# Cross attention on one core: the row maximum of a score tile in the first pass, as one VectorE instruction over 128x1024 instead of two over 128x512

## The chip, the cores and the metric

The kernel runs on one core of one Trainium2 chip. The metric is the device time of one execution in microseconds (us), the median of the runs shown. A core has TensorE (PE; its weight loads are shown apart, as PEld), VectorE (DVE), ScalarE (ACT), GpSimd (POOL) and SyncE (SP, which here only issues DMAs), each with an instruction queue of its own that is worked through in order. Waits between engines are semaphore waits.

## The reference, cut to what matters

For 8 batches of 256 rows, 1024 wide, with 32 heads of 32 columns:

```python
mu, var = mean(x), var(x)                       # over the last axis
z = (x - mu) * rsqrt(var + 1e-5) * gamma + beta
Q = split_heads(z @ Wq.T)
K = V = split_heads(ctx)                        # ctx has 256 rows too
scores = einsum('bhsd,bhtd->bhst', Q, K) * 32 ** -0.5    # masked
probs = softmax(scores)
attn = einsum('bhst,bhtd->bhsd', probs, V)
out = x + merge_heads(attn) @ Wout.T
```

## The kernel before, in words

Every matmul input but the probabilities is split into two f16 parts, and products are made from three partial ones (PASSES). The batches b0 to b7 are worked through one after the other. The work of a batch is two passes over the scores.

**The first pass** finds, for every row of scores, the logarithm of its sum of exponentials. It has 16 steps (STEPS). In step n, TensorE makes one score tile of 128 query rows x 4 heads x 256 keys (scores_s, matmuls at L588) in the PSUM tensor score[n % 2], so there are two buffers. VectorE finds the maximum of each row and head (max_step, L912 to L918), negated, into nmax. ScalarE takes the exponential of the tile with nmax as bias and accumulates the sums, one ACTIVATE for each of the 4 heads, each followed by an ACTIVATION_READ_ACCUMULATOR (row_sums, L733 to L741). The last of them releases sum_done, and scores_s of step n+2 waits for it at L582 before it overwrites the buffer.

**What fills TensorE between score tiles** is written out by hand. From b1 on, behind the scores of each step stand 7 matmuls of the output projection of the batch before (o_matmuls, L560, 128x512 each; 6 in b7), and near the end of the pass some of the query projection of the next batch (q_matmuls, L514, 128x256 each): 4 in step 13, 18 in step 14, and 38 behind the scores of step 15. In b0 there are query projections and the transposes of Wout (wo_transposes, L477; ScalarE's part of them is L724, VectorE's L832).

**VectorE's other work in the first pass**: the residual adds of the output (add_residual, L962) behind the maxima of steps 5, 8, 11 and 14; lse_half in step 10; and lse_rows, five dependent small instructions (L943 to L951), behind the maximum of step 12. They turn the sums of the first 8 steps into three rows of l_rows, which SyncE's queue puts into q_stack by DMA (fill_l_rows, L262). In that queue they stand behind loads, stores and the DMA transposes of the next batch (turn_z L230, turn_k L237).

**The second pass** makes the transposed scores with the logarithm already in the matmul (scores_t, L614), so that one ACTIVATE over 128x1024 gives the probabilities (exp_step, L761), then the product with V (probs_times_v, L626) and its split (att_split: L769 on ScalarE, L955 on VectorE). Its first two tiles wait for sum_done of steps 14 and 15 and for the DMAs of l_rows.

max_done counts the maxima: two per step, so row_sums waits for it ahead of head 0 and ahead of head 2 (L737, L738), and lse_half for all of its half (L923).

Of the kernel before, what the change touches and what calls it, by code (L numbers as in the profile page):

```python
# [13 lines left out]
AX = mybir.AxisListType  # L14
# [19 lines left out]
STEPS = G * ST  # L34
# [14 lines left out]
def xattn(nc, x, ctx_in, mask, wq, wout, gamma, beta, out):  # L49
    es = ExitStack()  # L50
    with es:
        def sb(name, shape, dt):
            return es.enter_context(nc.sbuf_tensor(name, shape, dt))

        def sem(name):
            return es.enter_context(nc.semaphore(name))
# [18 lines left out]
        nmax = sb("nmax", [P, ST, 2, J, HALF], F32)  # L75
# [58 lines left out]
        score = [es.enter_context(nc.psum_tensor(f"score{i}", [P, J, S], F32)) for i in range(2)]  # L134
# [26 lines left out]
        s_ready, max_done, sum_done = sem("s_ready"), sem("max_done"), sem("sum_done")  # L161
# [532 lines left out]
        def _(act):  # L694
# [38 lines left out]
            def row_sums(b, n):  # L733
                g, st = n // 2, n % 2
                h, gl = divmod(g, HALF)
                for j in range(J):
                    if j % 2 == 0:  # L737
                        act.wait_ge(max_done, b * 2 * STEPS + 2 * n + j // 2 + 1)  # L738
                    last = act.activation(score[n % 2][:, j, :], score[n % 2][:, j, :], ACT.Exp, bias=nmax[:, st, h, j, gl:gl + 1],  # L739
                                          accum_out=sums[:, st, h, j, gl:gl + 1])  # L740
                last.then_inc(sum_done, 1)  # L741
# [29 lines left out]
            def iteration(b, first, last):  # L771
                for n in range(STEPS):
                    if first and n in Q0_SPLITS:
                        q_split(0, Q0_SPLITS[n])
                    if first and n == Q1_SPLIT:
                        q_split(1, 0)
                    row_sums(b, n)
                    if first:
                        wo_split(n)
                    if n == STEPS // 2:  # L780
                        ln_sums(b, 0)
                    if n == STEPS // 2 + 1:
                        exp_ln(b, 0)
                ln_sums(b, 1)
                exp_ln(b, 1)
                splits = Q_SPLITS_FIRST if first else Q_SPLITS
                for g in range(G):
                    if not last and g in splits:
                        q_split(b + 1, splits[g])
                    exp_step(b, 2 * g, first, last)  # L790
                    exp_step(b, 2 * g + 1, first, last)
                    if g >= 2:
                        att_split(b, g - 2, first)
                att_split(b, G - 2, first)
                if not last:
                    q_split(b + 1, 3)
                att_split(b, G - 1, first)
# [21 lines left out]
        def _(dve):  # L819
# [92 lines left out]
            def max_step(b, n):  # L912
                g, st = n // 2, n % 2
                h, gl = divmod(g, HALF)
                dve.wait_ge(s_ready, b * STEPS + n + 1)
                for j2 in range(2):
                    at = slice(2 * j2, 2 * j2 + 2)
                    dve.tensor_reduce(nmax[:, st, h, at, gl], score[n % 2][:, at, :], AX.X, ALU.max, negate=True).then_inc(max_done, 1)  # L918


            def lse_half(b, h):
                at = b * 6 + 3 * h
                dve.wait_ge(max_done, b * 2 * STEPS + (h + 1) * STEPS)  # L923
                dve.wait_ge(ln_done, b * 2 + h + 1)
                dve.scalar_tensor_tensor(out=lse_t[:, :, h], in0=nmax[:, :, h], scalar=1.0, in1=ln_s[:, :, h], op0=ALU.mult, op1=ALU.subtract).then_inc(lse_step, 1)
                dve.wait_ge(le_done, b * 2 + h + 1)
                dve.scalar_tensor_tensor(out=lse_r[:, :, h], in0=sums[:, :, h], scalar=1.0, in1=ln_e[:, :, h], op0=ALU.mult, op1=ALU.mult).then_inc(lse_step, 1)
                dve.wait_ge(lse_step, at + 2)
                for st in range(ST):
                    last = dve.scalar_tensor_tensor(out=lse[:, st, h], in0=lse_t[:, st, h], scalar=1.0, in1=lse_r[:, st, h], op0=ALU.add, op1=ALU.subtract)  # L930
                last.then_inc(lse_step, 1)
# [33 lines left out]
            def iteration(b, first, last, more):  # L965
                adds = O_ADDS_LAST if last else O_ADDS
                for n in range(STEPS):
                    max_step(b, n)
                    if first and n in Q0_SPLITS:
                        q_split(0, Q0_SPLITS[n])  # L970
                    if first and n == Q1_SPLIT:
                        q_split(1, 0)
                    if first and n == 0:
                        centre(1, 0)
                    if first and n in (1, 2):
                        normalise(1, n - 1)
                    if first and n > 0:
                        wo_split(n - 1)
                    if not first and n in adds:
                        if adds.index(n) == 0:  # L980
                            if known(b, 1):
                                dve.wait_ge(k_in[1], 4 * DMA)
                            else:
                                for i in range(2):
                                    dve.wait_ge(out_done[i], (b - 1) * 2 * DMA)
                        add_residual(b - 1, adds.index(n))
                    if n == STEPS // 2 + 2:
                        lse_half(b, 0)
                    if n == L_STEP + 1:
                        lse_rows(b, 0)  # L990
# [3 lines left out]
                if first:  # L994
                    wo_split(STEPS - 1)
                lse_half(b, 1)
                for g in range(G):
                    if not last and g in splits:
# [83 lines left out]
```

## Time and profile before

| What | Value |
|---|---|
| Median of 3 runs | 584.61 us (583.23, 584.61, 587.07) |
| The profiled execution's own time | 582.48 us |
| Its span, first to last instruction | 580.6 us, so 1.9 us lie around it |
| PE busy (matmul) | 547.9 us, 94% of the span |
| ACT busy | 427.0 us, 74% |
| DVE busy | 370.3 us, 64% |
| POOL busy | 186.7 us, 32% |
| Mean granted TensorE clock | 0.994 of full speed |

The profile is of one execution, with times from the start of its span. A row of the timeline reads: start in us, length in us, engine, line of the kernel, operation, output <- inputs, shapes, how many instructions are merged in the row (x4), and in brackets the idle time of the engine before it with what ended it. Matmuls are pipelined, and the ends of their rows are modelled.

### The profile page before, as it was taken

What the parts mean: (1) busy time and instruction counts of PE and PEld (TensorE: products, weight loads), DVE (VectorE), ACT (ScalarE), POOL (GpSimd) and SP (SyncE); (2) the same over time, 40 slices, a digit from 0 to 9 for tenths busy, and PEclk for the clock granted to TensorE, in tenths of its full rate; (3) what the DMA queues carried; (4) which work ended last, traced back from release to release, by engine and by line L of the source; (5) the groups of instructions that cost most, each with busy time, mean ns of one, the idle gap of its engine ahead of it and who ended that gap; (6) DMA issues with size and microseconds to landing.
All of it is one profiled execution on the core that took longest, in us unless ns stands there. A gap on an engine that the chain in (4) does not pass through costs nothing.

```text
span 580.6 us, 12070 instructions
## 1 busy us (share of the span) xinstructions
PE 547.9 (94%) x4529; PEld 364.7 (63%) x4529; DVE 370.3 (64%) x751; ACT 427.0 (74%) x1322; POOL 186.7 (32%) x239
## 2 busy tenths in 40 slices
PE   1898799999999999999999999999999999999897
PEld 1787676556775577656775577656775577644443
DVE  4979687677647757478565857468565762278311
ACT  1469787698668975698668976598767986599850
POOL 0856530770047400590046400590036500030000
PEclk9999799999999999999999999999999999999999
DMA  8978992399128952299126972299325943031103
GB/s 311 314 190 232 246 197 85 96 218 207 39 73 143 226 144 80 68 233 237 45 73 133 225 153 76 42 200 258 87 73 126 221 93 89 24 91 56 58 2 109
DMA packets 122634, 80.90 MB, mean 139 GB/s; under 512 B 102000, under 2 KB 103568, under 8 KB 122576
## 3 DMA queue, kind: packets, MB, share of 16 engines
q1 hardware_dynamic: 119120, 73.84, 53.5%
q0 software_dynamic: 3456, 6.30, 6.0%
q8 instruction: 36, 0.59, 0.4%
q14 instruction: 22, 0.18, 0.1%
HBM read 34.61 MB, written 8.39 MB: 74 GB/s over the span
## 4 chain that ended last, share of the span: by engine, by line
PE 67%; SPq 8%; DVE 8%; POOL 6%; DMA 5%; ACT 4%; issue 2%; DVEq 0%
PE mm L514 21%; PE mm L560 15%; PE pv L626 11%; PE score L614 10%; PE score L588 6%; SPq L237 6%; ACT score L739 3%; DVE nmax L918 2%; PE mm L539 2%; PE score L539 2%; POOL probs L404 2%; DMA l_rest<-in_mask_BxS_bf 1%; DMA q_stack<-l_rows 1%; DMA ctx_sb<-in_ctx 1%; POOL probs L401 1%
## 5 line engine op out<-in xcount | busy, mean ns | idle before, releaser
L739 ACT ACTIVATE score<-score,nmax 128x256 f32<-128x256 f32 x512 | 230.0, 463 | 26.9 <-DVE nmax L918 26.0
L918 DVE TENSOR_REDUCE nmax<-score 128x2 f32<-128x512 f32 x256 | 164.2, 685 | 46.6 <-PE score L588 45.6
L514 PE MATMUL mm<-zT,wqT 128*128 128x256 f16 x1536 | 184.9, 273 | 1.6 <-DVE l_rows L951 1.1
L761 ACT ACTIVATE probs<-score 128x1024 f32<-128x1024 f32 x128 | 123.9, 1022 | 74.0 <-PE score L614 74.0
L514 PEld LDWEIGHTS mm<-zT,wqT 128*128 128x128 f16 x1536 | 149.8, 98 | 24.3 <-issue 4.2
L560 PE MATMUL mm<-woT,aT 128*128 128x512 f16 x672 | 161.5, 379 | 0.0
L739 ACT ACTIVATION_READ_ACCUMULATOR score<-score,nmax 128x1 f32 x512 | 113.6, 222 | 0.0
L560 PEld LDWEIGHTS mm<-woT,aT 128*128 128x128 f16 x672 | 65.4, 97 | 58.5
L588 PE MATMUL score<-k_stack,q_stack 97*128 97x256 f16 x512 | 78.6, 276 | 7.4 <-DMA q_stack<-qT 4.3
L955 DVE TENSOR_TENSOR aT<-pv,aT 128x256 f16<-128x256 f32 x64 | 26.9, 423 | 91.1 <-ACT aT L769 90.0
L378 POOL CAST z_nat<-x_nat 128x1024 f16<-128x1024 f32 x12 | 12.4, 1036 | 210.7 <-DVE x_nat L909 210.7
L588 PEld LDWEIGHTS score<-k_stack,q_stack 97*128 97x128 f16 x512 | 48.0, 98 | 39.4 <-issue 9.4
L614 PE MATMUL score<-q_stack,k_stack 100*128 100x256 f16 x512 | 67.8, 274 | 4.0 <-DMA q_stack<-l_rows 2.9
L626 PE MATMUL pv<-probs,ctx_sb 128*32 128x256 f32 x1024 | 68.5, 385 | 0.2 <-DVE aT L955 0.2
L411 POOL DMA_DIRECT2D q_stack<-qT x84 | 41.2, 498 | 75.8 <-DVE qT L847 75.6
L614 PEld LDWEIGHTS score<-q_stack,k_stack 100*128 100x128 f16 x512 | 45.4, 98 | 31.2 <-issue 17.7
L626 PEld LDWEIGHTS pv<-probs,ctx_sb 128*32 128x32 f32 x1024 | 26.9, 109 | 24.9 <-ACT probs L761 7.6
L731 ACT ACTIVATE qT<-mm 128x512 f16<-128x512 f32 x32 | 19.4, 608 | 14.2 <-PE mm L514 14.2
L769 ACT ACTIVATE aT<-pv 128x256 f16<-128x256 f32 x64 | 24.8, 390 | 6.6 <-PE pv L626 6.6
L847 DVE SCALAR_TENSOR_TENSOR qT<-mm,qT 128x512 f16<-128x512 f32 x32 | 22.1, 690 | 11.7 <-ACT qT L731 11.0
L404 POOL TENSOR_TENSOR probs<-ctx_sb,probs 128x512 f16<-128x512 f32 x24 | 27.5, 1148 | 0.0
L380 POOL TENSOR_TENSOR z_nat<-x_nat,z_nat 128x1024 f16<-128x1024 f32 x12 | 25.6, 2131 | 1.0
(96 smaller groups left out, 367.3 us busy)
## 6 DMA issues: line engine op xcount, KB each, us to landing
ctx_sb<-in_ctx SPq DMA_DIRECT2D x8, 1024.0 KB, 5.8
res<-in_x SPq DMA_DIRECT2D x32, 256.0 KB, 3.2
out<-o_buf SPq DMA_DIRECT2D x32, 256.0 KB, 2.5
x_nat<-in_x SPq DMA_DIRECT2D x6, 1024.0 KB, 6.0
q_stack<-qT SPq DMA_DIRECT2D x84, 64.0 KB, 2.0
q_stack<-qT POOLq DMA_DIRECT2D x84, 64.0 KB, 7.7
woT<-in_L_xattn_Wq SPq DMA_DIRECT2D x8, 512.0 KB, 12.5
probs<-in_L_xattn_Wout SPq DMA_DIRECT2D x8, 512.0 KB, 4.2
```

What stands on the lines that cost most here:

```text
L237: sp.dma_start_transpose(k_turned(pa, c), k_nat(a, c).rearrange("p n d -> p (n d)")).then_inc(k_in[c // 2], DMA)
L404: pool.tensor_tensor(to[:, :, 2 * DH:3 * DH], of, to[:, :, 0:DH], ALU.subtract).then_inc(k_done, 1)
L411: pool.dma_start(q_stack[DH * r:DH * (r + 1), 1, j], qT[DH * j:DH * (j + 1), part, HALF:G, :]).then_inc(q_in[1], DMA)
L514: last = pe.matmul(mm[i % 2][:, m2 * S:(m2 + 1) * S], wqT[:, wp, k, m * P:(m + 1) * P], zT[:, zp, k, :], start=(v2 == 0), stop=(v2 == KT * ...
L560: last = pe.matmul(mm[i % 2][:], aT[:, ap, k, st * P:(st + 1) * P], woT[:, wp, k, nh * 512:(nh + 1) * 512], start=(v == 0), stop=(v == O_M ...
L588: last = pe.matmul(score[n % 2][:, j, :], q_stack[0:S_ROWS, h, j, gl, st * P:(st + 1) * P], k_stack[0:S_ROWS, pb, h, gl, j, :], start=True ...
L614: last = pe.matmul(score[n % 2][:, j, :], k_stack[0:T_ROWS, pb, h, gl, j, tt * P:(tt + 1) * P], q_stack[0:T_ROWS, h, j, gl, :], start=True ...
L626: last = pe.matmul(pv[g % 2][DH * j:DH * (j + 1), 0, :], ctx_sb[:, pb, tt, g * P + DH * j:g * P + DH * (j + 1)], probs[:, g % 2, tt, j, :] ...
L739: last = act.activation(score[n % 2][:, j, :], score[n % 2][:, j, :], ACT.Exp, bias=nmax[:, st, h, j, gl:gl + 1], accum_out=sums[:, st, h, ...
L761: act.activation(probs[:, g % 2, tt], score[n % 2][:], ACT.Exp).then_inc(exp_done, 1)
L918: dve.tensor_reduce(nmax[:, st, h, at, gl], score[n % 2][:, at, :], AX.X, ALU.max, negate=True).then_inc(max_done, 1)
L955: dve.tensor_tensor(aT[:, 1, g, :], pv[g % 2][:, 0, :], aT[:, 0, g, :], ALU.subtract).then_inc(a_lo, 1)
```

## The change

The two reductions of a step become one over the whole tile. max_done then counts one per step, ScalarE waits once per tile ahead of head 0, and lse_half's count is halved.

```diff
             def row_sums(b, n):
                 g, st = n // 2, n % 2
                 h, gl = divmod(g, HALF)
+                act.wait_ge(max_done, b * STEPS + n + 1)
                 for j in range(J):
-                    if j % 2 == 0:
-                        act.wait_ge(max_done, b * 2 * STEPS + 2 * n + j // 2 + 1)
                     last = act.activation(score[n % 2][:, j, :], score[n % 2][:, j, :], ACT.Exp, bias=nmax[:, st, h, j, gl:gl + 1],
                                           accum_out=sums[:, st, h, j, gl:gl + 1])
                 last.then_inc(sum_done, 1)
...
                 dve.wait_ge(s_ready, b * STEPS + n + 1)
-                for j2 in range(2):
-                    at = slice(2 * j2, 2 * j2 + 2)
-                    dve.tensor_reduce(nmax[:, st, h, at, gl], score[n % 2][:, at, :], AX.X, ALU.max, negate=True).then_inc(max_done, 1)
+                dve.tensor_reduce(nmax[:, st, h, :, gl], score[n % 2][:], AX.X, ALU.max, negate=True).then_inc(max_done, 1)
 
 
             def lse_half(b, h):
                 at = b * 6 + 3 * h
-                dve.wait_ge(max_done, b * 2 * STEPS + (h + 1) * STEPS)
+                dve.wait_ge(max_done, b * STEPS + (h + 1) * STEPS // 2)
```

## Rows read from the trace of the kernel before

**Rows 1.** Busy time by engine, first pass of b3 (243.3 to 278.0 us)

```profile
core 0: us, PE busy (x) PEld busy (x) DVE busy (x) ACT busy (x) POOL busy (x), PEclk, DMA share, GB/s
243.30:278.00 34.70, 34.52 (x225) 21.36 (x222) 26.43 (x50) 31.65 (x134) 16.55 (x24) 1.00 1.01 213
```

**Rows 2.** Timeline, a steady step of b3's first pass and the step after next

```profile
256.98 0.60 PE L588 MATMUL score<-k_stack,q_stack 97*128 97x256 f16 x4
...
257.62 1.29 DVE L918 TENSOR_REDUCE nmax<-score 128x2 f32<-128x512 f32 x2 [0.66 <-PE score L588]
...
258.35 0.45 ACT L739 ACTIVATE score<-score,nmax 128x256 f32<-128x256 f32 x1
...
260.06 0.21 ACT L739 ACTIVATION_READ_ACCUMULATOR score<-score,nmax 128x1 f32 x1
...
260.67 0.53 PEld L588 LDWEIGHTS score<-k_stack,q_stack 97*128 97x128 f16 x4
...
260.88 0.60 PE L588 MATMUL score<-k_stack,q_stack 97*128 97x256 f16 x4
```

**Rows 3.** Groups of instructions by shape, whole kernel (count, busy us, mean ns)

```profile
L739 ACT ACTIVATE score<-score,nmax 128x256 f32<-128x256 f32 x512 | 230.0, 463 | 26.9 <-DVE nmax L918 26.0
L918 DVE TENSOR_REDUCE nmax<-score 128x2 f32<-128x512 f32 x256 | 164.2, 685 | 46.6 <-PE score L588 45.6
...
L761 ACT ACTIVATE probs<-score 128x1024 f32<-128x1024 f32 x128 | 123.9, 1022 | 74.0 <-PE score L614 74.0
...
L955 DVE TENSOR_TENSOR aT<-pv,aT 128x256 f16<-128x256 f32 x64 | 26.9, 423 | 91.1 <-ACT aT L769 90.0
```

**Rows 4.** Timeline, start of b3's first pass: maxima of step 0, scores of step 2

```profile
244.20 1.28 DVE L918 TENSOR_REDUCE nmax<-score 128x2 f32<-128x512 f32 x2
...
247.22 0.60 PE L588 MATMUL score<-k_stack,q_stack 97*128 97x256 f16 x4
```

**Rows 5.** Timeline, steps 13 to 15 of b3's first pass

```profile
270.91 2.47 DVE L918 TENSOR_REDUCE nmax<-score 128x2 f32<-128x512 f32 x4
...
271.62 0.45 ACT L739 ACTIVATE score<-score,nmax 128x256 f32<-128x256 f32 x1 [1.37 <-DVE nmax L918]
...
273.34 0.21 ACT L739 ACTIVATION_READ_ACCUMULATOR score<-score,nmax 128x1 f32 x1
...
273.60 0.33 PEld L588 LDWEIGHTS score<-k_stack,q_stack 97*128 97x128 f16 x4 [0.46 <-ACT score L739]
...
274.05 4.31 PE L514 MATMUL mm<-zT,wqT 128*128 128x256 f16 x38
```

**Rows 6.** Timeline of PE, from the first pass to the second, b1

```profile
141.02 4.31 PE L514 MATMUL mm<-zT,wqT 128*128 128x256 f16 x38
145.44 1.05 PE L614 MATMUL score<-q_stack,k_stack 100*128 100x256 f16 x8
```

**Rows 7.** Timeline of PE, from the first pass to the second, b6

```profile
471.92 4.31 PE L514 MATMUL mm<-zT,wqT 128*128 128x256 f16 x38
476.07 1.04 PE L614 MATMUL score<-q_stack,k_stack 100*128 100x256 f16 x8
```

**Rows 8.** Chain that ended last: start us, us, what; end of b0's and of b7's first pass

```profile
76.12 1.93 ACT score L739 x8
...
83.93 1.93 ACT probs L761 x2
...
533.29 5.58 ACT score L739 x24
```

**Rows 9.** Timeline of b7's first pass: maxima of step 0, scores of steps 2 and 12, logarithm

```profile
507.44 1.28 DVE L918 TENSOR_REDUCE nmax<-score 128x2 f32<-128x512 f32 x2
...
510.14 0.61 PE L588 MATMUL score<-k_stack,q_stack 97*128 97x256 f16 x4
...
528.62 0.60 PE L588 MATMUL score<-k_stack,q_stack 97*128 97x256 f16 x4
...
538.89 0.23 ACT L745 ACTIVATE ln_s<-sums 128x32 f32<-128x32 f32 x1
```

## The prediction, made before the changed kernel was run

> **What bounds the kernel now.** I read the page first (TensorE busy 94% of the span, so the question is where TensorE will wait), then the busy time by stretch, the timeline of one step, and the chain that ended last. In the first pass of b3 TensorE is busy 34.52 of 34.70 us, ScalarE 31.65, VectorE 26.43 [rows 1]: TensorE is the bound, ScalarE is close behind, VectorE has room. The reader is to see in the timeline that the three form a loop. The scores of a step start at 256.98, the maxima 0.64 later at 257.62, ScalarE at 258.35, 0.73 after them and thus as soon as the first of the two is done; the step's last accumulator read ends at 260.27, and the scores two steps on, which need that buffer, start at 260.88 with a weight load at 260.67 [rows 2]. So two steps take 3.90 us on TensorE, and the buffer is free 0.40 us before the weight load. That is the slack of the loop that the change draws on.
>
> **The new instruction.** The trace has no reduction over 1024. The one over 512 takes 685 ns [rows 3]; two back to back end 1.29 us after the first began [rows 2], so the second adds 0.605. From 256 to 512 columns VectorE grows from 423 to 685 ns [rows 3], 262 per 256, so 1024 gives 0.685 + 2 x 0.262 = 1.21 us. That beats the pair (1.29) by 0.08 us: per step VectorE gains that. Bounds: below, ScalarE's instruction over 128x1024 takes 1.02 [rows 3]; above, two full durations, 1.37. I take 1.21, since it extends the same engine's own rows.
>
> **What it adds.** ScalarE now waits for all of the maxima. Its start moves from 0.73 to 1.21 + 0.05 = 1.26 after the maxima begin: 0.53 later (bounds 0.34 and 0.69). Behind that wait stand the four ACTIVATEs of the step, and for the last of them the scores two steps on. The removed second wait gains nothing: it never held ScalarE, whose starts in a tile are 0.45 us apart throughout.
>
> **The loop, anew.** From ScalarE's start to the end of its last read is 260.27 - 258.35 = 1.92 us [rows 2]. Where TensorE had to wait, the weight load followed the last read by 0.05 (273.34 + 0.21 to 273.60 [rows 5]), the scores start with it (0.01 later), and the maxima begin 0.64 after the scores [rows 2], together 0.65. Two steps need 1.26 + 1.92 + 0.05 + 0.65 = 3.88 us. TensorE's own work gives 3.90. The loop is just covered in b1 to b6, and in b7, where a step has 6 filling matmuls and takes 1.82 to 1.84 us because of ScalarE, it is not. The places one by one:
>
> *Start of b1 to b6.* VectorE comes late to step 0, from the end of the batch before. Maxima at 244.20, so the buffer is free at 244.20 + 1.26 + 1.92 + 0.05 = 247.43, against scores that start at 247.22 [rows 4]: +0.2 per batch.
>
> *Steady steps, b1 to b6.* 3.88 against 3.90: nothing by the sum, but a weight load that comes that late is no longer hidden behind the matmul in front. I put 0.1 for a batch.
>
> *Steps 13 to 15, b1 to b6.* Here ScalarE already waits, 1.37 us, because lse_rows holds VectorE; and TensorE waits for ScalarE, 0.46 for the weight load at 273.60 [rows 5]. Nothing covers ScalarE's later start. Less the 0.05 to 0.08 that step 12's cheaper maximum gives back: +0.48. The end of ScalarE's sums also comes later, by 0.3 more, but behind the scores of step 15 TensorE has 38 matmuls (4.15 us), 1.5 us more than ScalarE needs. Hidden.
>
> So each of b1 to b6 loses 0.8 us on TensorE. Part of it was lost anyway: the second pass starts when l_rows is in q_stack, and in b1 TensorE was ready at 141.02 + 4.15 = 145.17 but started at 145.44 [rows 6], while in b6 it started at 471.92 + 4.15 = 476.07 without a wait [rows 7]. The same subtraction for the six batches gives waits of 0.27, 0.99, 0.38, 1.21, 0.14 and 0. SyncE's queue sets these; in the timeline it goes from one transpose to the next since the batch began and waits for none of VectorE's work that moves, so its end stays. Each delay is swallowed up to its wait: left are 0.5, 0, 0.4, 0, 0.7 and 0.8, together 2.4 us of 4.8.
>
> *b0.* VectorE itself sets its first steps; 3 maxima there and 2 later give 0.08 each back, 0.3 or 0.4. From step 13 the chain runs through ScalarE to the first probabilities (76.12 to 83.93) [rows 8], where the later start counts in full, 0.53. Net +0.2.
>
> *b7.* Step 0's maxima begin at 507.44, so the scores of step 2 start at 507.44 + 1.26 + 1.92 + 0.06 = 510.68 and not 510.14: +0.54. From step 2 to step 12 are five pairs: 5 x 3.88 = 19.40 against 528.62 - 510.14 = 18.48 [rows 9]: +0.9. At step 13 the chain goes through VectorE to ScalarE: +0.53, less 0.08. After that ScalarE did three tiles in one run (24 instructions, 5.58 us) [rows 8]; step 15 now needs sums of 13, scores, maxima, so its sums start 3.88 after those of 13, not 3.60: +0.3. Together +2.2, and the logarithm at 538.89 [rows 9] and all behind it move by that; nothing later in b7 absorbs it, as the second pass of b7 hangs on it.
>
> Sum: 0.2 + 2.4 + 2.2 = +4.8 us. The profiled execution's own 582.48 (span 580.6 and 1.9 around it) becomes 587.3. It lies 2.1 under the median of the runs, so the median 584.61 becomes 589.4.
>
> **A rule weighed.** The rows show VectorE not full (26.43 of 34.70) and ScalarE's start hanging on the first half-result [rows 1, 2]. The Trainium skill speaks to both sides in Perfetto Trace Analysis, section Optimizing Scalar/DVE Operations: grouping into larger operations helps where the engine is saturated; where it isn't, but causes bubbles on others, splitting lets work finish sooner. The trace agrees with the second for the steps of this pass; by the first, 128 x 0.08 = 10 us of VectorE's time would be the gain. That is the faster rival below, and its condition doesn't hold by these rows.
>
> **The rivals.**
> (a) *Every pair of steps waits.* If the late weight load costs 0.1 to 0.2 us for each pair, or the reduction takes 1.37, the loop is 4.0 to 4.05. Six pairs in six batches at 0.15 add 5.4; the swallowed part grows only to 3.0 in all. Time: +8 to +11, 593 to 596. For: the margin is 0.02 us, ScalarE gets 0.24 more in steps 8 and 9 and has only 0.14 us of room per step (1.95 less 4 x 0.45). Against: the one place where TensorE waits shows a restart at once.
> (b) *Hidden.* SyncE's chain ends later than in this execution (it moves by a us between batches) or the reduction takes nearer 1.02; then b1 to b6 lose next to nothing and b7 some 1 to 2: +1 to +2.5, 585.6 to 587.
> (c) *Faster.* VectorE is the real bound where it matters: if its end of step, not ScalarE's start, releases what is late, each of 128 steps gains up to 0.08: -10 us at most, and some -6 (578.5) if b1 to b6 alone do so. It decides where VectorE reaches the next maxima after the scores are ready. For: so it is in b0's first steps and behind lse_rows in step 12. Against: VectorE sat 45.6 us waiting for scores before these maxima [rows 3].
>
> **Chances.** Forecast, +3 to +7: 0.53. (a) 0.22, (b) 0.20, (c) 0.05. A measurement of this kernel can tell about 1% from no change, 5.8 us, up to 590.5. The forecast lies under it for some two thirds, (b) wholly, (a) not at all. So faster by over 1% 0.04, within 1% 0.58, slower by over 1% 0.38. The bounds of the reduction carried through the same sum give +1.4 (1.02) and +10.9 (1.37), so 586.0 to 595.5; the range is 585.6 to 595.
>
> **What would show it.** 128 reductions of some 1.21 us in place of 256 of 0.685, and VectorE's busy time for them down from 164 to 155 us. ScalarE's first ACTIVATE 1.26 after the maxima begin; its idle time behind nmax up from 26.9 us [rows 3]. In b1 to b6 the weight load of step 15 about 0.95 late against 0.46, the scores of step 2 0.2 later, the steps between still 1.95 apart; waits for l_rows shorter in b2 and b4. In b7 steps of 1.94. Wrong would be: steps of 1.98 or more in b1 to b6 (a), a first pass of b7 not longer (b), or score tiles that start earlier than before (c).

## The result, and the profile after

The changed kernel takes 588.35 us (median of 20 runs, 586.31 to 592.41) against 583.12 for the kernel before (20 runs); the ratio is 1.0083, 95% interval 1.0064 to 1.0102. So it is slower by 5.2 us, where +4.8 was forecast (588.35 us for 589.4). A ratio, here and below, leaves out single executions more than 1.5% above the fastest of their kernel, and is not the exact quotient of the medians. Its profiled execution took 589.48 us with a span of 587.6, 7.0 more than the span of before.

Groups of instructions of the changed kernel, from its page (count | busy us, mean ns | idle before them); they answer to [rows 3]:

```profile
L738 ACT ACTIVATE score<-score,nmax 128x256 f32<-128x256 f32 x512 | 229.5, 452 | 33.1 <-DVE nmax L915 29.7
L915 DVE TENSOR_REDUCE nmax<-score 128x4 f32<-128x1024 f32 x128 | 156.0, 1222 | 57.0 <-PE score L588 54.9
...
L588 PE MATMUL score<-k_stack,q_stack 97*128 97x256 f16 x512 | 78.6, 276 | 11.5 <-ACT score L738 6.7
...
L588 PEld LDWEIGHTS score<-k_stack,q_stack 97*128 97x128 f16 x512 | 43.3, 98 | 50.8 <-ACT score L738 32.1
```

The reduction over 1024 takes 1.222 us (1.21 was estimated), and VectorE's busy time for the maxima falls from 164.2 us [rows 3] to 156.0. None of it is gained: VectorE's idle time before the maxima rises by more, from 46.6 [rows 3] to 57.0. The weight loads of the score tiles now wait 32.1 us for ScalarE (8.9 in the kernel before), but most of that is hidden, as the weight load runs while TensorE is still busy with the matmuls in front. What costs time shows in the third line: the matmuls themselves stand idle for ScalarE for 6.7 us, where it was 2.2 us in the kernel before.

A steady step of b3's first pass, from the timeline of the changed kernel; it answers to [rows 2]:

```profile
250.28 0.60 PE L588 MATMUL score<-k_stack,q_stack 97*128 97x256 f16 x4
...
250.92 1.23 DVE L915 TENSOR_REDUCE nmax<-score 128x4 f32<-128x1024 f32 x1 [0.72 <-PE score L588]
...
252.18 0.45 ACT L738 ACTIVATE score<-score,nmax 128x256 f32<-128x256 f32 x1
...
254.17 0.34 PEld L588 LDWEIGHTS score<-k_stack,q_stack 97*128 97x128 f16 x4 [0.32 <-ACT score L738]
254.19 0.60 PE L588 MATMUL score<-k_stack,q_stack 97*128 97x256 f16 x4
```

ScalarE starts 252.18 - 250.92 = 1.26 us after the maxima begin (0.73 in [rows 2]). The weight load two steps on has moved from 0.21 ahead of its matmul to 0.02, yet the scores start 3.91 us after those two steps before: the loop just closes.

The two places of b1 to b6 where it doesn't, again in b3, timeline of the changed kernel; they answer to [rows 4] and [rows 5]:

```profile
245.08 1.22 DVE L915 TENSOR_REDUCE nmax<-score 128x4 f32<-128x1024 f32 x1
...
248.32 0.61 PE L588 MATMUL score<-k_stack,q_stack 97*128 97x256 f16 x4
```

```profile
272.04 0.60 PE L588 MATMUL score<-k_stack,q_stack 97*128 97x256 f16 x4
...
273.27 0.45 ACT L738 ACTIVATE score<-score,nmax 128x256 f32<-128x256 f32 x1 [1.30 <-DVE nmax L915]
...
275.25 0.33 PEld L588 LDWEIGHTS score<-k_stack,q_stack 97*128 97x128 f16 x4 [0.93 <-ACT score L738]
275.26 0.61 PE L588 MATMUL score<-k_stack,q_stack 97*128 97x256 f16 x4 [0.65 <-ACT score L738]
```

At the start the scores of step 2 come 248.32 - 245.08 = 3.24 us after the maxima of step 0, against 3.02 in [rows 4]. From step 14 to 15 it takes 3.22 us, and the weight load of step 15 waits 0.93 us against 0.46 [rows 5].

The distances of the score tiles, taken from the same timeline rows for every batch (us):

| | step 1 to 2 | 7 to 8 | 14 to 15 | other steps | step 0 to 15 |
|---|---|---|---|---|---|
| before, b1 to b6 | 1.95 | 1.95 | 2.75 | 1.95 | 30.3 |
| changed, b1 to b6 | 2.17 | 2.03 | 3.22 | 1.95 | 31.07 |
| before, b7 | 1.84 | 1.91 | 3.03 | mostly 1.82 | 28.72 |
| changed, b7 | 2.38 | 2.17 | 3.23 | mostly 1.83, 2.07 by turns | 30.83 |

("Step n to n+1" is from scores to scores; 12 comes 0.2 later in each for the two transposes before it.) Step 7 to 8 of b2 is left out, since there TensorE stood still for another reason, below.

Where the 7.0 us of the two spans come from, by the start of each batch's scores: -1.2 before b0's first scores, +0.5 in b0 (74.12 against 73.57), +3.9 in b1 to b6 (400.15 against 396.27), +2.4 in b7 to the logarithm (34.70 against 32.34), +1.4 behind it (43.12 against 41.68).

The last of these was in no term of the forecast. PE's timeline of the changed kernel, second pass of b7:

```profile
547.52 1.94 PE L626 MATMUL pv<-probs,ctx_sb 128*32 128x256 f32 x16
549.39 1.61 PE L614 MATMUL score<-q_stack,k_stack 100*128 100x256 f16 x8
```

Busy time of the changed kernel in two stretches (columns as in [rows 1]):

```profile
547.40:549.40 2.00, 2.00 (x18) 0.61 (x18) 0.71 (x2) 1.25 (x2) 0.00 (x0) 0.50 0.01 2
540.00:544.00 4.00, 2.52 (x14) 1.20 (x14) 2.21 (x3) 3.86 (x18) 0.00 (x0) 1.00 0.20 72
```

TensorE's granted clock is 0.50, the lower of its two levels (1.2 GHz), from about 547.4 on, and the 16 matmuls of the product with V take 1.94 us there and 1.07 elsewhere. Before that, from 540 to 544, TensorE was busy 2.52 of 4.00 us at full clock. But so it was in the kernel before: there it was busy 2.52 of the 4.00 us up to the logarithm (534.9 to 538.9), and no fall followed.

### The profile page after: what moved, and what is told of

The parts are those of the page before. It is cut to its first block, busy times and chain, and to the rows that moved or that the text cites. A ratio compares the mean times of both kernels' runs of the same rounds, so it can differ in the third digit from the quotient of the medians.

```text
span 587.6 us, 11942 instructions
## 1 busy us (share of the span) xinstructions
PE 551.7 (94%) x4529; PEld 360.5 (61%) x4529; DVE 363.1 (62%) x623; ACT 429.5 (73%) x1322; POOL 186.7 (32%) x239
## 4 chain that ended last, share of the span: by engine, by line
PE 59%; DVE 9%; POOL 9%; SPq 9%; ACT 7%; DMA 5%; issue 2%; DVEq 0%
PE mm L514 21%; PE pv L626 11%; PE score L614 10%; PE mm L560 9%; SPq L237 7%; ACT score L738 5%; PE score L588 4%; DVE nmax L915 4%; POOL probs L404 2%; POOL probs L401 2%; POOL q_stack L411 2%; PE mm L539 2%; PE score L539 2%; DMA ctx_sb<-in_ctx 1%; DMA l_rest<-in_mask_BxS_bf 1%
## 5 line engine op out<-in xcount | busy, mean ns | idle before, releaser
L915 DVE TENSOR_REDUCE nmax<-score 128x4 f32<-128x1024 f32 x128 | 156.0, 1222 | 57.0 <-PE score L588 54.9
L738 ACT ACTIVATION_READ_ACCUMULATOR score<-score,nmax 128x1 f32 x512 | 107.1, 209 | 0.0
L588 PEld LDWEIGHTS score<-k_stack,q_stack 97*128 97x128 f16 x512 | 43.3, 98 | 50.8 <-ACT score L738 32.1
```

The lines of the kernel that those rows point to most:

```text
L588: last = pe.matmul(score[n % 2][:, j, :], q_stack[0:S_ROWS, h, j, gl, st * P:(st + 1) * P], k_stack[0:S_ROWS, pb, h, gl, j, :], start=True ...
L915: dve.tensor_reduce(nmax[:, st, h, :, gl], score[n % 2][:], AX.X, ALU.max, negate=True).then_inc(max_done, 1)
```

## The experiments

All are built from the kernel before or the changed one. They ran on three chips (g4 on a fourth), e1 5 times, e4 6, g3 8 and the others 12 times; each ratio is against the kernel before on the same chip (medians there 582.29, 582.65 and 581.95). "By the medians" below is the plain difference to these.

**e1_pair_one_wait.** Two reductions, one wait of ScalarE for both:

```diff
                 for j in range(J):
-                    if j % 2 == 0:
-                        act.wait_ge(max_done, b * 2 * STEPS + 2 * n + j // 2 + 1)
+                    if j == 0:
+                        act.wait_ge(max_done, b * 2 * STEPS + 2 * n + 2)
```

> Two reductions of 512 as before, but ScalarE waits for both ahead of head 0. My theory (the loss is ScalarE's later start, not the wide instruction): ScalarE starts 1.34 us after the maxima begin, 0.08 later even than with the wide instruction, so two steps need 3.96 us against 3.90 of TensorE's work. Score tiles of b1 to b6 now come 0.06 later per pair of steps, the step after 14 is 3.3 long, b7's first pass is 0.4 longer still than the changed kernel's. Time: 2 us or so over the changed kernel, +6 to +9 over the kernel before. Rival (the instruction over two banks, or its length on VectorE, costs by itself): the kernel before's time, within 1 us.

591.12 us, ratio 1.0161 (1.0128 to 1.0194), +8.8 us by the medians. A step of b3, from its timeline:

```profile
249.32 1.29 DVE L918 TENSOR_REDUCE nmax<-score 128x2 f32<-128x512 f32 x2 [0.66 <-PE score L588]
...
250.65 0.45 ACT L739 ACTIVATE score<-score,nmax 128x256 f32<-128x256 f32 x1
250.67 0.33 PEld L588 LDWEIGHTS score<-k_stack,q_stack 97*128 97x128 f16 x4 [0.38 <-ACT score L739]
```

ScalarE starts 1.33 us after the maxima begin. Every second step is now 2.00 us, the last one 3.30, and a first pass of b1 to b6 takes 31.48. With the very instructions of the kernel before, and only the wait moved, the loss is larger than the change's own. So it comes from when ScalarE starts, not from the wide instruction; and a start 0.07 us later than with the wide one was enough to take the loop over its edge.

**e3_wide_covered, e4_wide_b7, e5_wide_0_13.** Three parts of the change, each alone. Here max_done was raised by the number of heads that a reduction covers:

```diff
+        def max_parts(b, n):
+            return (4,) if 1 <= b < B - 1 and n not in (0, 13) else (2, 2)
...
-                    dve.tensor_reduce(nmax[:, st, h, at, gl], score[n % 2][:, at, :], AX.X, ALU.max, negate=True).then_inc(max_done, 1)
+                    dve.tensor_reduce(nmax[:, st, h, at, gl], score[n % 2][:, at, :], AX.X, ALU.max, negate=True).then_inc(max_done, part)
```

(b == B - 1 in e4, 1 <= b < B - 1 and n in (0, 13) in e5.)

> The wide reduction only in b1 to b6, and there not in steps 0 and 13; pairs elsewhere. Theory: the loop's 3.88 us lies just inside TensorE's 3.90, so only step 8 (where ScalarE's logarithm stands) gives 0.08 per batch: +0 to +0.5 over the kernel before, score tiles 1.95 apart. Rival (each pair of steps pays for the late weight load): +3 or more. Rival (VectorE's saved time pays): -2 or lower.

> The wide reduction only in b7. Theory: b7's first pass up to the logarithm takes 2.4 us longer, as in the changed kernel, and nothing else moves; in addition TensorE's granted clock falls to half for some 3 us behind it, as in the changed kernel's profile, for 1.5 more: +2.4 to +3.9. If the halved clock in that profile was chance and has nothing to do with the longer waits of TensorE there: +2.4. Rival (the loss is in b1 to b6 alone): +0.

> The wide reduction only in steps 0 and 13 of b1 to b6. Theory: 0.2 and 0.47 us on TensorE in each of the six batches, 4.0 in all, of which the wait for the rows of l_rows swallows a part: +1.5 to +3 over the kernel before. Rival (swallowed wholly, as SyncE's queue is the bound there): +0 to +0.5. Together with the other two parts it makes the changed kernel's +5.2 if the parts add.

In this order: 584.35 us, ratio 1.0034 (1.0009 to 1.0059); 588.92, 1.0131 (1.0090 to 1.0172); 584.81, 1.0047 (1.0024 to 1.0071). These don't tell the parts apart, because they brought a change of their own: also where two reductions stood, the maxima began 0.71 us after the scores and not 0.64. From the timeline of e4_wide_b7, b3, where it should be the kernel before:

```profile
248.19 0.60 PE L591 MATMUL score<-k_stack,q_stack 97*128 97x256 f16 x4
...
248.90 1.29 DVE L925 TENSOR_REDUCE nmax<-score 128x2 f32<-128x512 f32 x2 [0.66 <-PE score L591]
```

In e3 this made every second steady step 2.00 us. They are a second sight of the edge that e1 showed: with 0.07 us more in the loop, here ahead of the maxima and there behind them, it is longer than TensorE's work.

e5 lies in its range (+2.5 us by the medians); e3 doesn't (+2.1, for +0.5 at most), by its steps of 2.00 us. e4 was slower than any of its expectations: +6.6 us by the medians, where at most +3.9 was expected. Its profiled execution, at 585.54 us the fastest of the six, has 35.16 us in b7 up to the logarithm and a halved clock behind it, and its span is 3.0 us longer than that of before. Why the other five took 588 to 594 us no trace shows; f1 below, the same part with increments of one, doesn't repeat it.

**g4_pair_inc2.** The kernel before with every increment of max_done and every wait on it doubled, one execution:

```diff
-                    dve.tensor_reduce(nmax[:, st, h, at, gl], score[n % 2][:, at, :], AX.X, ALU.max, negate=True).then_inc(max_done, 1)
+                    dve.tensor_reduce(nmax[:, st, h, at, gl], score[n % 2][:, at, :], AX.X, ALU.max, negate=True).then_inc(max_done, 2)
```

> The kernel before with max_done raised by two per reduction and all waits on it doubled; nothing else. If the 0.07 us more from scores to maxima in the runs with increments above one comes from the increment, it is here too: 0.71 us and not 0.64, and 128 more instructions in the profile (12198). Rival (it came from the mixed widths of those kernels): 0.64 and 12070. In time no difference that one execution can show.

585.25 us beside 578.95, one run each, which settles nothing about time (its b5 held one stall of 3.4 us, below). What the increment does is plain in its timeline:

```profile
251.67 0.60 PE L588 MATMUL score<-k_stack,q_stack 97*128 97x256 f16 x4
252.38 1.29 DVE L918 TENSOR_REDUCE nmax<-score 128x2 f32<-128x512 f32 x2 [0.66 <-PE score L588]
```

Again 0.71 us, and its span lists 12198 instructions against 12070: one more for each of the 128 steps. It is the wait for the scores, which now is an instruction of its own (an EVENT_SEMAPHORE, x128) ahead of the first reduction of a step. With the increment above one comes that instruction, and 0.07 us more between the scores and the maxima.

**f1_wide_b7, f2_wide_0_13, f3_wide_covered.** The same three parts with increments of one, and the counts worked out by a function:

```diff
+        def wide(b, n):
+            return b == B - 1
+
+        def maxima(b, n):
+            return sum(1 if wide(*divmod(i, STEPS)) else 2 for i in range(b * STEPS + n))
...
+                    if j == 0 or j == 2 and not wide(b, n):
+                        act.wait_ge(max_done, maxima(b, n) + j // 2 + 1)
...
+                for at in (slice(0, 4),) if wide(b, n) else (slice(0, 2), slice(2, 4)):
+                    dve.tensor_reduce(nmax[:, st, h, at, gl], score[n % 2][:, at, :], AX.X, ALU.max, negate=True).then_inc(max_done, 1)
```

> The wide reduction only in b7, now with increments of one so that VectorE's wait for the scores stays within its instruction (the maxima must begin 0.64 us after the scores, not 0.71 as in the runs with increments above one). Theory: b7 from its first scores to the logarithm 2.4 us longer, the pairs of steps 3.90 apart; and if the halved clock behind it follows from TensorE's longer waits there, up to 1.5 more: +2.4 to +4. Rival (the clock falls there in the kernel before just as often): +2.4. Rival (the loss is in b1 to b6): 0.

> The wide reduction only in steps 0 and 13 of b1 to b6, with increments of one. Theory: step 2 comes 0.21 later and step 15 0.47 later, as in the changed kernel, 4.1 in all on TensorE, of which the wait for l_rows takes a part: +1.5 to +3. Rival (swallowed wholly by SyncE's queue): +0 to +0.5.

> The wide reduction only in b1 to b6 and there not in steps 0 and 13, with increments of one. Theory: two steps need 3.90 us and TensorE's work gives 3.90, so the steps stay 1.95 apart but for 0.08 at step 8: within 0.5 of the kernel before. Rival (late weight loads cost in every pair): 2.00 in every second step, +2 or more.

| | median us | ratio (95%) | where the wide one stands | elsewhere |
|---|---|---|---|---|
| f1_wide_b7 | 583.33 | 1.0027 (0.9993 to 1.0060) | b7, scores to logarithm, 34.70 us | b1 to b6 30.3, as before |
| f2_wide_0_13 | 584.43 | 1.0031 (1.0010 to 1.0052) | 2.17 and 3.28 us, first pass 31.06 | b7 32.36, as before |
| f3_wide_covered | 580.41 | 0.9984 (0.9957 to 1.0012) | 2.03 at step 7 to 8, else 1.95; 2.68 at 14 to 15 | b7 32.37 |

By the medians they are +0.7, +1.8 and -2.2 us. In the traces the parts are clean. b7 alone costs 34.70 - 32.34 = 2.36 us. Steps 0 and 13 alone cost 31.06 - 30.30 = 0.76 on TensorE in each of six batches. The steps in between cost nothing: TensorE loses 0.08 at step 8 and gets 0.07 back at step 15, because VectorE is through step 12 sooner. (A finer split, one reduction per head, was not tried.) In time only the second part is clear of zero. f1's ratio gives +1.6 us, where at least +2.4 was expected, with an interval up to +3.5; the three ratios add up to +0.42% where the whole change is +0.83%. So the times don't contradict the traces, and don't prove the split either. The three leave out b0.

**f6_wide_filled.** The changed kernel with 6 matmuls more in b7, whose results are thrown away:

```diff
                 for g in range(G):
                     scores_t(b, pb, 2 * g)
+                    if last and g == 0:
+                        for _ in range(6):
+                            pe.matmul(pv[0][:].rearrange("p c s -> p (c s)"), aT[:, 0, 0, 0:P], woT[:, 0, 0, 0:512], start=True, stop=True)
                     scores_t(b, pb, 2 * g + 1)
```

> The changed kernel with 6 more matmuls of 512 columns in b7, between the first and the second transposed score tile, where TensorE otherwise waits 1.2 us for ScalarE's sums (their results are thrown away). If the halved clock behind it in the changed kernel's profile comes from TensorE's waits there, it is gone: 1 to 1.5 us under the changed kernel, so +3.5 to +4.5 over the kernel before, and the product with V behind the gap takes 1.0 us and not 1.9. Rival (the fall comes at a time of its own or from something else): the changed kernel's +5 or the extra matmuls' own time on top, up to +5.5.

586.98 us, ratio 1.0099 (1.0067 to 1.0130), +4.3 us by the medians. Its PE timeline in b7:

```profile
541.51 1.46 PE L662 MATMUL pv<-woT,aT 128*128 128x512 f16 x6
...
545.77 1.07 PE L626 MATMUL pv<-probs,ctx_sb 128*32 128x256 f32 x16
```

The product with V takes 1.07 us here and the rest behind the logarithm 41.68, so in this execution there was no fall of the clock. But its ratio isn't lower than the changed kernel's (1.0083, and 1.0114 in g3 below). And the fall doesn't need the change: f3_wide_covered has pairs in b7, and its PE timeline shows

```profile
541.80 1.94 PE L632 MATMUL pv<-probs,ctx_sb 128*32 128x256 f32 x16
```

while f1_wide_b7 has the wide reduction there and none. Without the filled one, the halved stretch stands behind b7's first pass in 5 of the 6 profiles where ScalarE waits for the whole tile in b7, and in 4 of the 7 where it doesn't. It costs 0.9 to 2.4 us (42.5 to 44.1 us behind the logarithm against 41.7). Whether the change makes it more frequent is open, and whether the filling ever prevents it, one profile can't say.

**f4_wide_late_rows, f5_pair_late_rows.** lse_rows behind the maximum of step 13, from b1 on, in the changed kernel and in the one before:

```diff
-                    if n == L_STEP + 1:
+                    if n == L_STEP + (1 if first else 2):
                         lse_rows(b, 0)
```

> The changed kernel with lse_rows behind the maximum of step 13 and not 12, from b1 on. ScalarE's start at step 13 then hangs on the scores and not on VectorE's five small instructions; the maxima of step 14 come 1.4 us late instead, which the 18 and 38 matmuls of TensorE cover. Theory: from the scores of step 14 to those of step 15 TensorE needs 2.4 us, its own work, against 3.22 in the changed kernel, so each of b1 to b6 gains 0.8 where SyncE's rows don't hold the second pass: 1.5 to 4 us under the changed kernel. The wait at step 2 (0.21) and the steps of b7 stay. Rival (the late start costs at step 13 wherever lse_rows stands): the changed kernel's time.

> The kernel before (two reductions) with the same move of lse_rows. Theory: 2.4 against 2.75 us from step 14 to 15 in b1 to b6, 2.1 us in all on TensorE, half of it lost to the wait for l_rows; b7 gains up to 1: 0.5 to 2.5 under the kernel before. The distance between one reduction and two in b1 to b6 shrinks from 0.77 to 0.3 us a batch. Rival (SyncE's queue bounds every batch, nothing gained): the time before.

f4: 584.31 us, ratio 1.0040 (1.0013 to 1.0067), 4.5 us under the changed kernel on the same chip (g3). f5: 582.46, 1.0004 (0.9979 to 1.0030). Steps 14 to 15 take 2.41 us in both, TensorE's own work: with lse_rows out of the way the wide reduction's late result costs nothing at step 13, and a first pass of b1 to b6 takes 30.25 with it and 29.95 with pairs; 0.77 us of difference have become 0.30. But the kernel before gains nothing from it. PE's rows of f5 in b3:

```profile
269.75 4.32 PE L514 MATMUL mm<-zT,wqT 128*128 128x256 f16 x38
...
275.32 1.05 PE L614 MATMUL score<-q_stack,k_stack 100*128 100x256 f16 x8 [1.26 <-DMA q_stack<-l_rows]
```

TensorE is ready sooner and waits for SyncE's rows: 1.26, 1.05 and 1.22 us in b3 to b5, and 2.21 in b7. That is the swallowing of the forecast, seen from the other side. So f5's expectation of 0.5 to 2.5 us gained failed, and its rival, that SyncE's queue takes it all, held. Nor does b7 gain: the logarithm there comes 0.6 us later than before (32.92 for 32.34).

**g3_changed_again.** The changed kernel, beside f4 and f5:

> The changed kernel once more, beside the others on one chip: +4 to +6.5 over the kernel before, the same steps (2.17, 2.03, 3.22 us) in b1 to b6. Open is whether its second profile shows the halved clock in b7 again: if it comes from the change's longer waits it should; if it is chance, as the two profiles with pairs in b7 that showed it say, it may or may not.

588.80 us, ratio 1.0114 (1.0072 to 1.0156), +6.9 us by the medians, with the same steps (2.17, 2.03, 3.21 or 3.22) and b7's 34.68 us. The halved clock is there again.

## Why the prediction was right

*The new instruction.* 1.21 us was forecast and it takes 1.222. The 262 ns per 256 columns came from two different operations, though (a TENSOR_TENSOR over 256 and a reduction over 512 [rows 3]); that a reduction grows by as much (from 685 to 1222 ns it is 268 per 256) these rows couldn't show.

*The mechanism.* ScalarE's start 0.53 us later was put as the whole cost. It does start that much later (1.26 for 0.73), and e1, which keeps both reductions and only delays ScalarE, loses more than the change does. The faster rival (c) fell: VectorE did save 8 us, and they stand in its idle time.

*The loop at 3.88 against 3.90.* From the scores to the weight load that ScalarE released it measures 254.17 - 250.28 = 3.89; where TensorE had to wait, the scores followed their weight load by 0.01 (275.25 to 275.26), so the loop is 3.90, level with TensorE's own 3.90. The margin was forecast at 0.02 us and is about nothing: that the steady steps cost nothing is right, but by less than the sum could tell. e1 and e3 show how near it was: 0.07 us more made two steps 3.96. Rival (a), where every pair of steps waits, was 0.07 us away and not a wrong idea; the late weight load itself cost nothing (0.02 us ahead of its matmul, and 1.95 a step). The 0.1 put for the steady steps came out as the 0.08 of step 8, but not because each late weight load costs something, for which it was put, nor by ScalarE's longer work in steps 8 and 9, which rival (a) named. The timeline of g3_changed_again in b3, the weight load of step 7, ScalarE's last read of the buffer that step 8 needs, and the weight load of step 8:

```profile
259.14 0.34 PEld L588 LDWEIGHTS score<-k_stack,q_stack 97*128 97x128 f16 x4 [0.31 <-ACT score L738]
...
260.83 0.22 ACT L738 ACTIVATION_READ_ACCUMULATOR score<-score,nmax 128x1 f32 x1
...
261.16 0.34 PEld L588 LDWEIGHTS score<-k_stack,q_stack 97*128 97x128 f16 x4 [0.38 <-issue]
```

The read ends at 261.05, and the load follows 0.11 later, where it otherwise follows by 0.05. So some 0.3 of its 0.38 us is the wait for ScalarE as in step 7, and the last 0.06 or 0.07 is a wait for nothing that the profile shows, at the very place of the stalls in the last section. In the kernel before, the same weight load is 0.21 ahead of its matmul like the others:

```profile
258.72 0.53 PEld L588 LDWEIGHTS score<-k_stack,q_stack 97*128 97x128 f16 x4
...
258.93 0.60 PE L588 MATMUL score<-k_stack,q_stack 97*128 97x256 f16 x4
```

So the size was right and the reason half right: the lead of the weight loads is gone, as forecast, but it costs only at the one step where something else delays the load.

*The terms.*

| term | forecast | measured |
|---|---|---|
| start of b1 to b6, each | +0.2 | +0.22 |
| steady steps, each | +0.1 | +0.08 |
| step 15, each | +0.48 | +0.47 |
| b7 up to the logarithm | +2.2 | +2.36 |
| b0, its first steps | -0.3 or -0.4 | +0.38, then swallowed |
| b0, from step 15 on | +0.53 | +0.54 |
| b1 to b6 net of the wait for l_rows | +2.4 | +3.9 in the first pair of profiles; see below |

*b0.* The whole came to +0.5 in the first pair, for +0.2, and the first half of the reasoning fails. The steps 0 to 7 were to get shorter, as VectorE sets them; they take 17.64 us and not 17.26, in every profile of the changed steps 0.4 longer (the distances ahead of steps 2, 5, 6 and 7 grow, those ahead of 3 and 4 shrink). It costs nothing there, because TensorE waits for a DMA of q_stack at step 8 in any case: 3.73 us, where it was 4.30. The second half holds: from the scores of step 15 to b1 it takes 31.48 us and not 30.94, and all nine profiles with pairs in b0 lie at 30.93 to 30.95, the four with the changed steps at 31.47 or 31.48. So b0 costs the full 0.5.

*What was swallowed.* On TensorE b1 to b6 lose 0.77 us each, 4.6 in all. The waits for l_rows, taken by the forecast's subtraction, were 3.0 us in the kernel before and 2.8 in the changed kernel's first profile, so there next to nothing was swallowed in sum: b2 and b4 wait less, as forecast (0.37 and 0 for 1.0 and 1.2), but b1 and b3 wait 1.5 and 1.0. In g3_changed_again they are 0.7 in all, in f6_wide_filled 0.2. Over all profiles with pairs in b1 to b6 and lse_rows in its place (before, f1, e4, g4: 3.0, 1.9, 2.8, 3.1) and the three of the changed steps (2.8, 0.7, 0.2) the mean falls from 2.7 to 1.2: some 1.4 us swallowed, where 2.4 was forecast. From the first scores of b1 to those of b7 it took 400.15, 397.47 and 398.72 us in the three profiles of the changed steps, and 396.27 and 394.19 in the two of the old steps (f1 is the second): 398.8 and 395.2 in the mean, +3.6 (e4 has the old steps there too but for 0.06 us in each pass: 395.9). The stalls between steps 7 and 8 (1.0 us in b2 of the kernel before, 0.45 in b2 of the changed one, 1.56 in b5 of f6) stand in profiles of both; without them it is +3.4, against +2.4 forecast. So a part is swallowed, as forecast, but the term was a us too small: it took SyncE's end from one execution as fixed ("its end stays"), and from run to run the second pass of a waiting batch begins up to 2 us earlier or later (b1: 35.16 us after its first scores in the kernel before, 37.12 in the changed one, 35.41 in f1).

*What was missed.* The halved clock behind b7, +1.4 us in the profiled pair; and the stall at step 8, in the kernel before 1.0 us in b2. In the median the sum came out at +5.2 for +4.8, and part of that closeness is luck: the term for b1 to b6 was a us too small and that for b0 0.3, the clock was in no term, and the single runs scatter by 6 to 7 us in either kernel.

*The rule weighed.* The Trainium skill, Perfetto Trace Analysis, section Optimizing Scalar/DVE Operations, says that grouping can raise throughput where the engine is saturated, and that splitting may let work finish sooner where it isn't but causes bubbles on others. The runs agree with its second half in steps 0 and 13 and in b7 (0.76 and 2.36 us lost by grouping). In the covered steps, where no bubble follows, neither matters (f3, 0.9984).

No version tried here is faster than the kernel before beyond the noise: f3 has the lowest time, 580.41 us, but its interval (0.9957 to 1.0012) holds 1.

## What to carry to other kernels

Where two small instructions let their consumer start on the first half, merging them saves their overhead but delays the consumer: count the loop from the producer's start to the buffer's release and compare it with the work that hides it, in each stretch where either changes. Here a loop of 3.90 us, level with TensorE's own 3.90, cost nothing, one of 3.96 cost 0.05 a pair of steps, and where TensorE waited for ScalarE already the whole 0.5 counted. What becomes late first is found at the irregular steps (the first, the one behind a chain of small instructions, the last batch with less filling), not at the average.

## What the runs showed that was not expected

With a semaphore increment above one on VectorE's reductions, their wait for the scores became an instruction of its own, one more per step (12198 for 12070), and 0.07 us came between the scores and the start of the maxima (0.71 for 0.64, g4_pair_inc2). It was enough to make a covered loop an uncovered one (e3_wide_covered).

TensorE's granted clock fell to 0.50 near the end of the first pass of b7 or behind it in 9 of 14 profiles, with pairs and with the wide reduction alike, and in 11 of the 14 TensorE had been busy the same 2.52 of the last 4.00 us before the logarithm: 7 of these show the fall and 4 (before, e3, f1, g4) don't. What decides is open. In b0 it stands at 0.50 for 3.4 to 10.2 us in all 14, around step 8, where TensorE waits some 4 us for a DMA.

Between the scores of steps 7 and 8 TensorE stands still for 0.4 us or more in b2 or b5 (once in b1) in 11 of the 14 profiles, with all it needs long done. From the PE timeline of g4_pair_inc2, b5:

```profile
393.19 0.60 PE L588 MATMUL score<-k_stack,q_stack 97*128 97x256 f16 x4 [3.26 <-issue]
```

The scores before it started at 387.82, so the step took 5.37 us and not 1.95. In this stretch the DMA engines were full (share 1.08) and one packet of an instruction queue was under way. That TensorE waited for its instructions would fit, but is not shown: the DMA engines are as full over the whole first pass of b3 [rows 1], and in b2 and b5 such a packet is under way near this step in profiles without a stall too (f1 and g3 in both batches).
